# Four-step units in three PSUM banks for the second graph layer of a GNN kernel

## What is computed

```python
edge_index = jnp.stack([src, dst])            # row = src, col = dst
deg = jax.ops.segment_sum(jnp.ones(col.shape), col, num_segments=n)
deg_inv_sqrt = jnp.where(deg > 0, jax.lax.rsqrt(deg), 0)
norm = deg_inv_sqrt[row] * deg_inv_sqrt[col]
msgs = norm[:, None] * x[col]
agg = jax.ops.segment_sum(msgs, row, num_segments=n)
out = agg + (1.0 + eps[0]) * x
...
x = _layernorm(x + _L1_gnn_ref(x, L1_gnn_eps, edge_index), axis=-1)
```

## Time and profile before

| | |
|---|---|
| median of 3 runs | 8717.58 us (8713.29 to 8717.87) |
| the profiled execution | 8707.91 us, its span 8706.1 us |
| PE busy | 6202.1 us (71%) |
| DVE busy | 5376.6 us (62%) |
| ACT busy | 3768.3 us (43%) |
| POOL busy | 6245.2 us (72%) |

### The profile page before, as it was taken

One profiled execution on the slowest core, in us unless ns is written; L12 is line 12 of the kernel. 1 busy time (PEld: TensorE's weight loads), 2 busy tenths in 40 slices (PEclk: granted clock), 3 DMA queues, 4 the chain that ended last, 5 costly groups with the idle time before them and its releaser, 6 DMA issues. The chain is left out here.

```text
span 8706.1 us, 153774 instructions
## 1 busy us (share of the span) xinstructions
PE 6202.1 (71%) x41943; PEld 5309.4 (61%) x41944; DVE 5376.6 (62%) x10966; ACT 3768.3 (43%) x8055; POOL 6245.2 (72%) x6523
## 2 busy tenths in 40 slices
PE   5788888888869999999634444444446777777776
PEld 2566666657769898999633333333336666666665
DVE  8898898888877888877722222222225555555554
ACT  5445355342052222222422222222236777777775
POOL 3677777777757766777477777777767777777774
PEclk7899999998789999999866666666668888888887
DMA  1122122121142222222222222222223443334432
GB/s 35 43 52 52 51 52 52 51 52 49 44 130 63 57 52 54 54 56 55 77 64 64 60 64 60 64 64 60 64 64 105 110 110 110 108 110 109 111 108 71
DMA packets 575365, 611.58 MB, mean 70 GB/s; under 512 B 114414, under 2 KB 472474, under 8 KB 574618
## 3 DMA queue, kind: packets, MB, share of 16 engines
q0 software_dynamic: 203776, 417.74, 18.9%
q1 hardware_dynamic: 294120, 145.77, 5.8%
q10 hardware_dynamic: 76722, 38.13, 1.5%
HBM read 562.68 MB, written 38.51 MB: 69 GB/s over the span
## 5 line engine op out<-in xcount | busy, mean ns | idle before, releaser
L2014 POOL DMA_INDIRECT M<-in_x,ixb x1664 | 1696.3, 1019 | 538.5 <-issue 530.0
L2195 PE MATMUL ps<-M,oh 128*128 x7056 | 1285.8, 349 | 1064.5 <-ACT M L2550 1034.1
L2061 POOL DMA_INDIRECT M<-t,ixb x1664 | 1615.7, 971 | 503.9 <-issue 498.1
L2195 PEld LDWEIGHTS ps<-M,oh 128*128 128x128 f32 x7056 | 1194.0, 253 | 1240.1 <-issue 1176.3
L2061 POOL DMA_INDIRECT M<-x,ixb x1664 | 1577.5, 948 | 503.9 <-issue 503.1
L2014 POOL DMA_INDIRECT M_any<-t,ixb x1376 | 1302.3, 946 | 501.1 <-issue 445.4
L1435 ACT ACTIVATE oht<-oneh,ot 128x128 f16<-128x128 f16 x3264 | 965.3, 387 | 979.6 <-DVE oneh L1411 979.6
L2213 DVE TENSOR_TENSOR acc<-acc,ps 128x1024 f32 x294 | 357.9, 1217 | 1587.5 <-PE ps L1776 1587.5
L1954 DVE TENSOR_TENSOR acc<-acc,ps 128x774 f32 (+1 forms) x988 | 942.7, 954 | 570.7 <-PE ps L1776 542.5
L2550 ACT ACTIVATE M<-M,wD 128x128 f32<-128x128 f32 x1664 | 517.1, 388 | 1488.2 <-DMA M<-x,ixb 1473.2
L1924 PEld LDWEIGHTS ps<-M,oh 128*128 128x128 f32 x5928 | 894.5, 209 | 266.0 <-issue 160.3
(11 more groups left out here) (306 smaller groups left out, 9256.1 us busy)
## 6 DMA issues: line engine op xcount, KB each, us to landing
er<-in_edge_attr SPq DMA_DIRECT2D x414, 256.0 KB
M<-in_x,ixb POOLq DMA_INDIRECT x1664
M<-x,ixb POOLq DMA_INDIRECT x1664
M<-t,ixb POOLq DMA_INDIRECT x1664
M_any<-t,ixb POOLq DMA_INDIRECT x1376
x<-lay SPq DMA_DIRECT2D x48, 256.0 KB, 2.4
part<-x ACTq DMA_DIRECT2D x48, 256.0 KB, 4.6
lay<-in_x SPq DMA_DIRECT2D x24, 256.0 KB, 3.9
```

The source lines that it names most:

```text
L2014: e.indirect_dma_start(M1[:, m1_slot(s, t), :] if layer else M[:, t % RING, 0:P], None, table[0:rows, :], bass.IndirectOffsetOnAxis(ap=ixb ...
L2061: e.indirect_dma_start(M2[:, t % RING, :], None, table[:, :], bass.IndirectOffsetOnAxis(ap=ixb[:, t:t + 1], axis=0)).then_inc(s_g[n % 16], 16)
L2195: ins = e.matmul(ps_flat[:, bass.ds(slot * P, P)], oh[:, j, :], tile_at(M2, tile, P), start=False, stop=False)
```

## The change

In layer 1 a unit becomes four steps (`U4`) in one PSUM bank, with three buffers in the banks 0, 1 and 2 (`B4`): 741 units in place of 494. One matmul clears the bank's start on TensorE in place of two. The closing matmuls go: the last step's product carries the stop flag and signals `s_st`. The row product gets bank 3 to itself, stands ahead of the unit's clearing wait, waits until the last one-hot was made from that bank, and signals by a semaphore of its own, `s_row`; ScalarE's clearing no longer waits for a one-hot. The one-hots of steps are made three units ahead. Expansion products may stand behind the first three of each four steps. Since the unit's first block differs, `places` has five more operations and writes the first blocks into a new small table `first4`, which VectorE reads every four units. Pieces of the later tables come every fourth unit of four in place of every third of six. Layer 0 keeps its units.

```diff
+            U4, B4 = 4, 3
+            UNITS4 = KP // U4
+            assert SG == U4 * B4 and UNITS4 * U4 == KP
...
+            def piece_due(s, u):
+                return s >= PIECES_FROM and 0 <= u < UNITS4 - 1 and u % 4 == 0
...
-            PERIOD, X0 = KP / XT, KP // 2 - US * 2
+            PERIOD, X0 = KP / XT, KP // 2 - SG
...
-            ROW_UNIT = {int(due(x) // US) - 2: x for x in range(X_ALL)}
+            ROW_UNIT = {int(due(x) // U4) - B4: x for x in range(X_ALL)}
             assert len(ROW_UNIT) == X_ALL
 
-            def row_pe(e, x, b0):
+            def row_pe(e, x):
                 s, i = x // XT + 1, x % XT
                 e.wait_ge(s_gx, s)
-                return e.matmul(ps[:, b0 + 1, 2 * P:3 * P], gxf[:, s % 2, i:i + 1].to_broadcast([P, P]), ident[:, :], start=False, stop=False)
+                if x:
+                    e.wait_ge(s_ot, x)
+                e.matmul(ps[:, 3, 0:P], gxf[:, s % 2, i:i + 1].to_broadcast([P, P]), ident[:, :], start=True, stop=True).then_inc(s_row, 1)
...
+                e.wait_ge(s_row, x + 1)
                 if x >= 2:
                     e.wait_ge(s_xp, x - 1)
                 e.tensor_tensor(ot[:, x % 2, 0:WIN[s], :],
-                                ps[:, b0 + 1, 2 * P:3 * P].rearrange("p (a b) -> p a b", a=1).to_broadcast([P, WIN[s], P]),
+                                ps[:, 3, 0:P].rearrange("p (a b) -> p a b", a=1).to_broadcast([P, WIN[s], P]),
...
             def clear_act(e, u):
-                h = u % 2
-                e.wait_ge(s_add, ST0[1] + max(u - 1, 0) * US + 1)
-                if u - 2 in ROW_UNIT:
-                    e.wait_ge(s_ot, ROW_UNIT[u - 2] + 1)
-                e.activation(ps_flat[:, h * 1024:h * 1024 + US * P], zwin[:, 0:1].to_broadcast([P, US * P]), ACT.Copy).then_inc(s_clr, 1)
+                e.wait_ge(s_add, ST0[1] + max(u - B4 + 1, 0) * U4 + 1)
+                e.activation(ps[:, u % B4, :], zwin[:, 0:1].to_broadcast([P, U4 * P]), ACT.Copy).then_inc(s_clr, 1)
...
-            PLACES = 12 + 2 * ((GT + RG - 2) // RG)
+            PLACES = 17 + 2 * ((GT + RG - 2) // RG)
...
-                op(lambda: e.tensor_tensor(at, at, t, ALU.subtract))
                 op(lambda: e.tensor_tensor(at, at, c0, ALU.add))
+                op(lambda: e.tensor_tensor(blocks, iotaK[0:1, 0:KP], t, ALU.subtract))
+                op(lambda: e.tensor_scalar(blocks, blocks, float(NB - 1), None, ALU.min))
+                op(lambda: e.tensor_scalar(starts, every(blocks, U4), float(NB - U4), None, ALU.min))
+                op(lambda: e.tensor_tensor(blocks.rearrange("p (m w) -> p m w", w=U4), blocks.rearrange("p (m w) -> p m w", w=U4),
+                                           starts.rearrange("p (m w) -> p m w", w=1).to_broadcast([1, UNITS4, U4]), ALU.subtract))
+                op(lambda: e.scalar_tensor_tensor(at, blocks, float(PACK), at, ALU.mult, ALU.add))
+                op(lambda: e.tensor_scalar(row, row, 10, 10, ALU.logical_shift_right, ALU.logical_shift_left))
                 op(lambda: e.tensor_tensor(row, row, at, ALU.add))
...
-                        if more and j < (2 if h else US - 1):
-                            more(s * KP + m * SG + j, 1)
                     close_pe(e, b0).then_inc(s_st, US)
-                    if more:
-                        more(s * KP + m * SG + h * US + US - 1, KP)
...
+            def group4_pe(e, regs, s, m, more):
+                if m == 0:
+                    e.wait_ge(s_map, PLACES * (s + 1))
+                    load_pe(e, regs, 0, s * KP)
+                at, ready = steps_pe(e, regs, T - 1)
+                for h in range(B4):
+                    u, k = s * UNITS4 + B4 * m + h, s * KP + m * SG + h * U4
+                    if u in ROW_UNIT:
+                        row_pe(e, ROW_UNIT[u])
+                    e.wait_ge(s_clr, u + 1)
+                    e.matmul(ps[:, h, 0:P], zwin[:, 0:1].to_broadcast([P, P]), ones_b[:, :], start=True, stop=False)
+                    if h == 0:
+                        e.wait_ge(s_arr, ready + (s * T + ARR0 + TILES))
+                    e.wait_ge(s_oh, OH0[1] + u + 1)
+                    for j in range(U4):
+                        tile, slot = at[h * U4 + j]
+                        ins = e.matmul(ps_flat[:, bass.ds(slot * P + h * 512, P)], oh[:, h * U4 + j, :], tile_at(M1_any, tile, P),
+                                       start=False, stop=j == U4 - 1)
+                        if j < U4 - 1:
+                            more(k + j, 1)
+                    ins.then_inc(s_st, U4)
+                    more(k + U4 - 1, KP)
+                    if h == B4 - 1 and m + 1 < KI:
+                        load_pe(e, regs, 0, s * KP + (m + 1) * SG)
+                    yield
...
+            def unit4_dve(e, regs, left, s, u):
+                if u == 0:
+                    e.wait_ge(s_map, PLACES * (s + 1))
+                if u % 4 == 0:
+                    n = min(4, UNITS4 - u)
+                    e.load(regs[0:n], first4[0:1, s % 2, u:u + n])
+                    left[:] = [e.snap(r, min_val=0, max_val=NB - U4) for r in regs[0:n]]
+                b = left.pop(0)
+                k0, h = s * KP + u * U4, u % B4
+                to = acc[:, bass.ds(b, U4), 0:P]
+                e.wait_ge(s_st, ST0[1] + k0 + U4)
+                e.wait_ge(s_add, ST0[1] + k0 + 1)
+                e.tensor_tensor(to, to, ps[:, h, :].rearrange("p (a b) -> p a b", b=P), ALU.add).then_inc(s_add, U4)
+                if s * UNITS4 + u in ROW_UNIT:
+                    row_dve(e, ROW_UNIT[s * UNITS4 + u])
+                batch(e, h, relS, k0 + SG, 6, U4)
...
-                    for u in range(UNITS):
-                        drain(unit_dve(e, 1, regs, left, s, u))
+                    for u in range(UNITS4):
+                        unit4_dve(e, regs, left, s, u)
                         if (s, u) == (0, 0):
                             stores_done(e, tal)
                             e.memset(raw_w[:, F * T:TILES], 0.0).then_inc(s_late, 1)
                             v(lambda: e.memset(gD[:, TILES:TILES + H], 0))
                         if (s, u) == (PIECES_FROM, 0):
                             e.wait_ge(s_ld, NLATE)
-                        if s >= PIECES_FROM and u % 3 == 0:
+                        if piece_due(s, u):
                             next(pieces, None)
-                        if s + 1 < SUP and u == 6:
+                        if s + 1 < SUP and u == 9:
                             window_rows(e, s + 1)
-                        if s + 1 < SUP and u == 20:
+                        if s + 1 < SUP and u == 30:
                             places(e, tm, s + 1)
...
-                            if s >= PIECES_FROM and (2 * m + h) % 3 == 1:
+                            if piece_due(s, B4 * m + h - 1):
```

More of the change, by code:

```diff
@@ L1810, in expand_pe @@
                     for w in range(WIN[s]):
-                        yield due(x) + (2 * PERIOD - 2 * US) * w / WIN[s]
+                        yield due(x) + (2 * PERIOD - SG) * w / WIN[s]
                         if w == 0:
@@ L1850, in expand_act @@
                 x = 0
-                for u in range(U_ALL):
+                for u in range(U_ALL4):
                     clear_act(e, u)
@@ L1933, in group_pe, with batch @@
                     yield
-            def batch(e, u, rel, k, bank):
-                e.tensor_tensor(oh[:, u * US:u * US + US, :],
-                                ps[:, bank, 0:P].rearrange("p (a b) -> p a b", a=1).to_broadcast([P, US, P]),
-                                rel[:, k:k + US].rearrange("p (a b) -> p a b", b=1).to_broadcast([P, US, P]),
+            def group4_pe(e, regs, s, m, more):
[23 more added lines that the diff above has]
+                    yield
+            def batch(e, u, rel, k, bank, n=US):
+                e.tensor_tensor(oh[:, u * n:u * n + n, :],
+                                ps[:, bank, 0:P].rearrange("p (a b) -> p a b", a=1).to_broadcast([P, n, P]),
+                                rel[:, k:k + n].rearrange("p (a b) -> p a b", b=1).to_broadcast([P, n, P]),
                                 ALU.is_equal).then_inc(s_oh, 1)
@@ L1943, in blocks_dve, with unit_dve @@
                 left[:] = [e.snap(r, min_val=0, max_val=NB - span) for r in regs[0:n]]
-            def unit_dve(e, layer, regs, left, s, u):
+            def unit_dve(e, regs, left, s, u):
                 if u % 4 == 0:
@@ L2389, in period @@
                         sliced = False
-                        for _ in unit_dve(e, 0, regs, left, s, u):
+                        for _ in unit_dve(e, regs, left, s, u):
                             sliced = sliced or next(gen, SLICE) == SLICE
@@ L2431, in run_vector @@
                 e.wait_ge(s_v, tv.n)
-                for u in range(2):
-                    batch(e, u, relS, u * US, 6)
+                for u in range(B4):
+                    batch(e, u, relS, u * U4, 6, U4)
                 pieces = dst_tables(e, "v", tv, tp, ta)
                 for s in range(SUP):
```

(10 more changed lines are left out.)

51 lines of the change are left out of this document (21 added, 30 removed).

## The result

The kernel after takes **8805.31 us** (median of 4 runs, 8801.96 to 8806.43), the one before 8717.73 in the same comparison (8713.29 to 8718.48): ratio 1.0101, 95% interval 1.0083 to 1.0118. It is 88 us slower, outside the predicted range of 8652 to 8750. Its profiled execution took 8805.8 us, its span 8804.0.

A forecast was written before the change was run, and what follows sets the result against it. The prediction took TensorE's instruction stream (its sequencer) to bound layer 1. Its terms, -15 - 10 - 25 + 23 + 15 + 0 + 2 + 5 = -5 us, gave 8712 us for the median, range 8652 to 8750.

The forecast's parts named there:

- Rows: Layer 1's row product waits twice instead of once, each second wait an instruction of 51 ns, 288 times: +15 us.
- Pieces: TensorE's waits for VectorE at table pieces grow as the unit between shortens, 0.1 us a piece: +5 us.
- fourth rival: Each of 48 table pieces waits for a one-hot and a piece, +37 us: 8745 us, chance 0.14.
- table of places: VectorE's chained block once a supertile grows 1.8 us, shorter work around it gives that back: 0 us.
- Closings: Fewer closing and clearing matmuls on TensorE: -15 us, and -10 where eight products trail a unit.
- buffers: A third PSUM buffer lets banks be cleared ahead, so clearing no longer holds up the sequencer: -25 us.
- interleaving: 348 more expansion products stand behind a step on TensorE, each costing 0.065 us more: +23 us.
- second rival: The sequencer sets TensorE's pace, but placing expansions behind steps costs nothing: -28 us, 8690 us, chance 0.26.
- third rival: ScalarE's in-order queue keeps the third buffer from winning its 25 us: +20 us, 8738 us, chance 0.10.

The follow-up runs named there:

- late row: Row product moved from its unit's head to just ahead of the unit's last step, against the kernel after: 8735.60 us, ratio 1.0012 to the kernel before.
- all three: Kernel after with late row, table-of-places operations spread one per unit, and TensorE's table-piece part two units behind VectorE's: 8628.14 us, ratio 0.9892 to the kernel before.
- two buffers: Kernel after with late row and later TensorE pieces, a bank cleared only after the add two units before: 11442.08 and 11314.11 us on two slower chips.
- two edits of a few lines: Kernel before with the table-of-places operations spread over units and TensorE's part of a table piece one unit later: 8636.44 us, ratio 0.9908.
- second chip's base: Kernel after with late row and TensorE's part of a table piece one unit later, on a second slower chip: 11112.88 us, ratio 0.9959 to the kernel before.

## Why the prediction was wrong

**The step that failed is "Rows".** It said that `row_pe` "waits twice instead of once; a second wait is an instruction of 51 ns", and set +15. It priced the instruction and not what the wait holds. The order of the queues gave the sum: the one-hot is made behind its unit's add, so it is ready a unit (2.0 us), an add (0.7) and a one-hot (1.5) after its row product, 4.17 us by the order of time (3709.57 to 3713.74). Two units later, 4.4 us on (two thirds of 6.56), the next row product wants it, or sooner where the sequencer leads. The late row measures the step at 78 us in place of 15; by the table 42 quiet groups of two rows gave 0.88 each, 128 of one row 0.15, nine blocks 2.4 and 49 groups with pieces 0.07, 80 in all. Where a queue stands at a wait mattered more than how many waits it has. The 78 holds the 21 us of the blocks too, where the wait only prolonged a pause that was there before.

**Pieces** (+5) were mis-sized. With TensorE's part a unit later 42 us come back, and groups with a piece fall from 8.65 to 7.36. The prediction's price was sound, its count was not. Where a row's one-hot stood between the two parts it reckoned 3.45 us of VectorE against a unit of 2.0, so 1.45; it then took 0.1 a piece, as "most units have none". In the trace after, 20 of 49 pieces have one: all 20 waited, 17 of them 1.55 us on average and three, behind a block, 6.3 to 6.6. Of the other 29, 14 waited, 8.6 us in all. The starting figure was short as well: the 18.1 us are 13 waits and not 27, two of them (8.2 us) at a block, and the pieces' other waits bring the kernel before to 27 us, the one after to 55. The fourth rival had the size (+37) and the mechanism, a wait of one unit, which the change shortened to 2 us; its wait at every piece was too many. As the old kernel had waits at pieces too, the 42 us that the mend brings are not exactly the term; the table's 47 are the other reading.

**The table of places** (0) was sized right by its own terms, a longer block against shorter work behind it: with the row product's wait out of the way a block group takes 12.46 for 12.28 before. Its words "and no row in that unit" were true and beside the point; the row two units on was the one waited for. That the pause as a whole was worth 86 us was not seen, as no term asked what the block costs, only what the change makes it cost.

**Closings, buffers, interleaving** (-15 - 10 - 25 + 23 = -27) had the right sign. Quiet groups with the late row take 6.55 against 6.74 on average; taken for all 247, which is an estimate, 0.19 each is 47 us less. That is near -50, the sum without the interleaving's +23. Undone, the interleaving gives -4 and -12 us of 11.2 thousand, within the intervals: the second rival's "interleaving costs nothing" is likelier than +23, but neither is shown. A closing at 0.03 to 0.04 us, on those chips, is under the 0.07 of array time. Groups without expansions, where the prediction took 0.06 off for closings, did not get shorter (6.13 us before, 6.13 with the late row).

The third buffer's term has its own sign in the traces, on the faster chip. Between the two register operations around a group's first clearing, what exceeds 0.15 us sums to 31 us before (the prediction's 32), to 38 after, where the row product's wait had taken the clearing's place, and to 1 with the late row and with all three (the layer's first group left out). The pair of a group with the late row, for the 3401.9 and 3402.5 of the earlier trace rows:

```profile
L1775 PEldq FUSED_REGOPS  x1: 38/38/38, 3704.8 to 3704.8; - x1
L1947 PEldq FUSED_REGOPS  x1: 67/67/67, 3704.9 to 3704.9; - x1
```

So the sequencer's hold-up, which the prediction priced at 25 us, did go. How much time that gave back there stays open, as two buffers were only tried on the slower chips. On these the third rival is refuted by 201 to 226 us. The Trainium skill, "TensorE: Matmul & The Clock Gate", section "HAM oscillation — how this bites in real kernels", says of its one kernel that adding PSUM double-buffering "gave no further gain". Here, on those chips, one buffer less costs the time just given.

**What was right.** A group without expansions takes 6.12 to 6.17 us in all seven kernels of the table (forecast 6.1), so the sequencer bounds it and closings don't cost array time; the mean group between 3513 and 4175, forecast at 7.0, is 7.33 after and 6.86 with the late row; VectorE's 59 us more were covered in one-row groups, as their 6.71 shows. GpSimd's pace of 129 us a supertile ended the gains when the three mends were made.

The sum with measured terms, from before to after: rows +78, pieces +42, table +2, units -47, gives +75 of the 88 measured; the mends were measured one at a time and overlap at the block, so the terms are good to some 20 us.

## What to carry to other kernels

Price a new wait by the chain that signals it, counted in the units of the waiting loop: here 4.2 us against 4.4, which leaves next to nothing, and where it became a stall it also took the sequencer's lead. Count how often each case of a wait occurs before calling it rare: 20 of 49 pieces had the row's one-hot in between. Put a product with its own wait as late in its unit as its consumer allows, and a long chain on a shared engine in pieces between units. And before rebuilding units, mend the waits of the old ones: two edits of a few lines gave 0.9908, the units on top of them 0.9892.

## What the runs showed that was not expected

Idle time at the waiting instruction understates a wait in an in-order sequencer. In quiet groups with two rows 0.31 of the 0.90 us lost stands at the waiting product; 0.55 stands a unit later, at the head of the next group, whose table load (0.85 us) and address arithmetic had lost their cover. And a pause that moves from one instruction to another looks like a gain at the first: the fall of the waits for cleared banks from 39.7 to 19.7 us was one.

The two kinds of chip differ, as far as these traces show, in how late a signal arrives and hardly in how long an instruction takes. In the second chip's base an add on VectorE takes 0.69 us and a gather 944 ns, as on the faster kind, but the add of a unit whose last weight load ended before 4704.4 started 3.4 us later:

```profile
4703.88 0.30 PEld L1953 LDWEIGHTS ps<-M_any,oh 128*128 128x128 f32 x2
4704.10 0.30 PEld L1827 LDWEIGHTS ps<-xw,ot 128*128 128x128 f32 x2
```

```profile
4707.80 0.69 DVE L2000 TENSOR_TENSOR acc<-acc,ps 128x512 f32 x1 [4.09 <-PE ps L1953]
```

On the faster kind the add at 3711.66, shown above, started 0.15 us after its unit's last step product. Over all adds of layer 1 that VectorE waited for, that distance is 0.15 us at the median with the late row (347 adds) and 2.7 us in the second chip's base (344 adds, the middle eight tenths from 0.15 to 5.1). TensorE, which pauses more, also has a lower granted clock over the layer there, 0.89 for 0.97. Why the signals come late is open. With such delays a third buffer is worth 200 us and more, and mends that won 0.0092 won 0.0014.
